# A fused vision block on one core: by-key scores in four PSUM banks, by-query scores in three, and a new order of the attention slots

## What is computed

```python
h = tok(x)                      # gray, two 3x3 Scharr convolutions, sum of absolutes / 2
n = layernorm(h)
q, k, v = n @ Wq + bq, n @ Wk + bk, n @ Wv + bv      # each in heads (b, n, 16, 16)
q, k = einsum("bnhe,ei->bnhi", q, Wp), einsum("bnhe,ei->bnhi", k, Wp)
scores = einsum("bnhi,bmhi->bnhm", q, k) / 4
h = h + einsum("bnhm,bmhe->bnhe", softmax(scores), v)
m = layernorm(h)
r = m + 0.5 * (silu(layernorm2(m) @ W1 + b1) @ W2 + b2)   # W1: 256x1024, W2: 1024x256, dequantised
out = h + r
```

## Time and profile before

| | us |
|---|---|
| median of 3 runs | 332.61 (329.96 to 335.14) |
| the profiled execution, its own time | 327.95 |
| its span in the trace | 326.2 |
| PE / PEld / DVE / ACT / POOL busy | 294.4 / 228.7 / 212.6 / 165.2 / 131.6 |

### The profile page before, as it was taken

How to read it: one execution, slowest core, us unless ns; L and a number is a source line. 1 busy time by engine, 2 the same in 40 slices (tenths; PEclk the granted TensorE clock), 3 DMA queues, 4 the chain that set the end, 5 groups by cost and what they waited for, 6 DMA issues and landing times.

```text
span 326.2 us, 6219 instructions
## 1 busy us (share of the span) xinstructions
PE 294.4 (90%) x2280; PEld 228.7 (70%) x2280; DVE 212.6 (65%) x423; ACT 165.2 (51%) x304; POOL 131.6 (40%) x250
## 2 busy tenths in 40 slices
PE   0599999999999997999999999788899999999996
PEld 0478888787767655565666656455699889999985
DVE  8979794846999676786777987431682563552422
ACT  1581534533323774767677766647434434444450
POOL 7423241502000108655747454326548769800000
PEclk9999999999999999999999999889999999999999
DMA  6985059999999676948990000000000100100201
GB/s 218 303 243 176 0 197 281 166 212 356 216 375 285 241 255 136 171 84 269 181 186 14 3 0 3 2 0 1 2 0 2 64 3 0 64 2 0 66 0 64
DMA packets 27911, 39.49 MB, mean 121 GB/s; under 512 B 4314, under 2 KB 14826, under 8 KB 27882
## 3 DMA queue, kind: packets, MB, share of 16 engines
q1 hardware_dynamic: 27720, 38.96, 45.2%
q10 hardware_dynamic: 162, 0.15, 0.1%
HBM read 24.42 MB, written 14.68 MB: 120 GB/s over the span
## 4 chain that ended last, share of the span: by engine, by line
PE 74%; DVE 14%; issue 5%; ACT 4%; POOL 1%; ACTq 0%; DVEq 0%; POOLq 0%
PE bank L1130 41%; PE bank L1244 9%; PE bank L1222 8%; PE bank L1227 4%; ACT probs L1037 3%; DVE negmax L841 3%; PE bank L1201 3%; PE bank L1262 3%; DVE qk_l L831 2%; PE bank L1254 2%; PE bank L1270 1%; DVE gray L718 1%; PE bank L1152 1%; DVE xn L806 1%; PE bank L1167 1%
## 5 line engine op out<-in xcount | busy, mean ns | idle before, releaser
L841 DVE TENSOR_REDUCE negmax<-bank 128x2 f32<-128x512 f32 x128 | 79.8, 682 | 15.7 <-PE bank L1201 15.7
L1037 ACT ACTIVATE probs<-bank 128x512 f32<-128x512 f32 x128 | 69.5, 595 | 35.5 <-PE bank L1227 33.6
L896 DVE TENSOR_TENSOR y_l<-yf,y_h 128x512 fp32r<-128x512 f32 x32 | 23.7, 742 | 39.1 <-ACT yf L1065 39.0
L1062 ACT ACTIVATE y_h<-bank,b1col 128x512 fp32r<-128x512 f32 x32 | 22.1, 689 | 48.5 <-PE bank L1130 48.4
L1130 PE MATMUL bank<-w_h,y_h 128*128 128x256 f32 x128 | 36.9, 288 | 2.5 <-DVE y_l L896 2.1
L1244 PE MATMUL bank<-probs,vals 128*32 128x256 f32 x512 | 35.1, 391 | 3.7
L1222 PE MATMUL bank<-negrow,pick 48*128 48x512 f32 x128 | 31.9, 495 | 7.0 <-ACT probs L1037 7.0
L1130 PE MATMUL bank<-w_l,y_h 128*128 128x256 f32 x128 | 36.2, 282 | 0.0
L1130 PE MATMUL bank<-w_h,y_l 128*128 128x256 f32 x128 | 36.2, 282 | 0.0
L1130 PEld LDWEIGHTS bank<-w_h,y_h 128*128 128x128 f32 x128 | 24.4, 190 | 4.6 <-DVE y_l L896 3.6
L1222 PEld LDWEIGHTS bank<-negrow,pick 48*128 48x128 f32 x128 | 12.0, 184 | 20.7 <-ACT probs L1037 15.4
(11 more groups left out here) (147 smaller groups left out, 627.6 us busy)
## 6 DMA issues: line engine op xcount, KB each, us to landing
qk_parts<-qk_h SPq DMA_DIRECT2D x32, 256.0 KB, 9.9
xr<-in_x SPq DMA_DIRECT2D x8, 768.0 KB, 8.4
qs<-qk_parts SPq DMA_DIRECT2D x16, 384.0 KB, 6.2
ks<-qk_parts SPq DMA_DIRECT2D x16, 384.0 KB, 7.8
qk_parts<-qk_l SPq DMA_DIRECT2D x16, 256.0 KB, 10.1
wraw<-in_L_ffn_fc_q SPq DMA_DIRECT2D x4, 512.0 KB, 3.9
wscale<-in_L_ffn_fc_scales SPq DMA_DIRECT2D x4, 512.0 KB, 7.3
out<-osb SPq DMA_DIRECT2D x16, 128.0 KB, 1.8
```

The source lines that it names most:

```text
L841: eng.tensor_reduce(negmax[:, b % 2, u, v], entry_bank(key)[:, :].rearrange("p (t k) -> p t k", t=NT), AX.X, ALU.max, negate=True).then_in ...
L896: eng.tensor_tensor(y_l[:, p % 2, f], yf[:, n % 2], y_h[:, p % 2, f].bitcast(fp32), ALU.subtract).then_inc(s_y, 1)
L1037: eng.activation(probs[:, n % PBUF], p2[n % 3][:, :], ACT.Exp).then_inc(s_exp, 1)
L1062: eng.activation(y_h[:, p % 2, f], src, ACT.Silu, bias=b1col[:, f:f + 1])
```

## The change

1. `p2` gets four banks (3 to 6), the ring three (0 to 2, n % 3). By-key scores of slot s now wait for the exponentials of slot s - 2, both heads, no longer for the first head of slot s - 1. All ring entries, those in the front too, wait for entry n - 3.
2. One by-query group (and its two reductions) a slot, not two groups in the even one. In the even slot it stands ahead of the by-key scores, in the odd one behind them: PE's row of a round is by-query, by-key, by-key, by-query, value products.
3. `copy_av` of a group stands on ACT behind the exponentials of the odd slot in which PE makes the group, no longer one slot later.
4. DRAM holds each high part once: two stores a tile, not three, and twelve loads of 16 partitions per half pair, not four of 48. Bytes loaded are the same.
5. The four loads of `fc1` weights are issued behind the last stores, before slot 0 of SP's loop, and wait only for the two stores under `wscale`; POOL's first step waits for all four. Before, they were issued from slot 2 on.
6. `fc1` product 1 goes to bank 1 and product 2 to bank 3, the other way round; product 2 waits for the last exponential.

```diff
-        p2 = bank[4:7]
+        p2 = bank[3:7]
...
         for s in range(END):
-            if s % 2 == 0:
-                for k in (s + AHEAD, s + AHEAD + 1):
-                    if k < SLOTS:
-                        head_entries(k)
+            if s + AHEAD < SLOTS:
+                head_entries(s + AHEAD)
...
-                r = n % 4
+                r = n % 3
...
-                for part, src in enumerate(((qk_h, qk_l, qk_h), (qk_h, qk_h, qk_l))[op]):
-                    eng.dma_start(qk_dram[p, op, m * P:(m + 1) * P, part, :], src[:, i, :].bitcast(fp32)).then_inc(s_store[i], 16)
+                for part, src in enumerate((qk_h, qk_l)):
+                    eng.dma_start(qk_dram[p, op, part, m * P:(m + 1) * P, :], src[:, i, :].bitcast(fp32)).then_inc(s_store[i], 16)
...
-                r, op, v = p % 2, k // 2, k % 2
-                src = qk_dram[p, op, m * P:(m + 1) * P].rearrange("(u v d) s t -> v (d s) u t", v=2, d=D)[v]
-                eng.dma_start((qs, ks)[op][HALF * v:HALF * v + SPLIT, r, m * 4:(m + 1) * 4, :].bitcast(fp32), src).then_inc(s_load[r][m], 16)
+                r = p % 2
+                op, slot, v = k // 6, k // 2 % 3, k % 2
+                part = ((0, 1, 0), (0, 0, 1))[op][slot]
+                dst = (qs, ks)[op]
+                first = HALF * v + slot
+                src = qk_dram[p, op, part, m * P:(m + 1) * P, :].rearrange("(u v d) t -> v d u t", v=2, d=D)[v]
+                eng.dma_start(dst[first:first + SPLIT - 2:3, r, m * 4:(m + 1) * 4, :].bitcast(fp32), src).then_inc(s_load[r][m], 16)
...
+            wait_filled(eng, ("qkv", PAIRS - 1, 0))
+            for i in range(2):
+                eng.wait_ge(s_store[i], 32 * PAIRS)
+            for part in range(4):
+                load_ffn(0, part)
...
-                if s >= 4 and s % 2 == 0:
-                    copy_av((s - 4) // 2)
+                if s % 2 == 1 and 3 <= s < SLOTS - 1:
+                    copy_av((s - 3) // 2)
...
-                if n >= 2:
-                    eng.wait_ge(s_exp, n - 1)
+                if n >= 4:
+                    eng.wait_ge(s_exp, n - 2)
...
             for s in range(END):
+                if s % 2 == 0 and s + AHEAD < SLOTS:
+                    scores_by_query(s + AHEAD)
                 if s < SLOTS:
                     scores_by_key(s)
-                if s % 2 == 0:
-                    for k in (s + AHEAD, s + AHEAD + 1):
-                        if k < SLOTS:
-                            scores_by_query(k)
+                if s % 2 == 1 and s + AHEAD < SLOTS:
+                    scores_by_query(s + AHEAD)
```

More of the change, by code:

```diff
@@ L298, in vit_tower_kernel @@
         N3_AT = {SLOTS - 9: (0, 0), SLOTS - 7: (0, 1)}
-        F1_AT = {SLOTS + (-5, -3, -1, 0)[i]: (i // KE, i % KE) for i in range(4)}
-        F1_AT.update({SLOTS + 2 + i: (2, i) for i in range(KE)})
+        F1_AT = {SLOTS + (-5, -3, -1, 0, 2, 3)[i]: (i // KE, i % KE) for i in range(6)}
         entries = []
@@ L337, in vit_tower_kernel @@
             held[r] = key
-        in_b = [[key for key in entries if ebank[key] == r and not (key[0] == "n3" and key[1] >= 1)][-1] for r in range(4)]
+        in_b = [[key for key in entries if ebank[key] == r and not (key[0] == "n3" and key[1] >= 1)][-1] for r in range(3)]
         def entry_bank(key):
@@ L357, in vit_tower_kernel @@
         LN_AT = (SLOTS - 24, SLOTS - 10)
[L360 removed]
+        F1_BANKS = (2, 1, 3)
         N3_MADE = {FT * (p - 1) + kf: (p, kf) for p in range(1, PAIRS) for kf in range(KE)}
@@ L425, in _ @@
                 stored(0, m)
-                for k in range(4):
+                for k in range(12):
                     load_qk(0, m, k)
@@ L453, in _ @@
                             eng.wait_ge(s_p2, max(s, UNITS * (2 * p - 3) + 4 * (m + 1)))
-                            load_qk(p, m, k)
-                if s in (2, 3, 5, 6):
-                    if s == 2:
-                        wait_read(eng, ("qkv", PAIRS - 1, 5))
-                        for i in range(4):
-                            eng.wait_ge(s_store[i], 48 * PAIRS)
-                    eng.wait_ge(s_p2, s)
-                    load_ffn(0, (2, 3, 5, 6).index(s))
+                            for i in range(3 * k, 3 * k + 3):
+                                load_qk(p, m, i)
                 if s in (23, 24):
@@ L600, in w1_step @@
                     eng.wait_ge(s_wraw, 16 * 4)
+                    if k == 0:
+                        for j in range(4):
+                            eng.wait_ge(s_store[j], 32 * PAIRS)
                     link(eng.tensor_scalar(full, wraw[:, cols], -128.0, 1.0, ALU.add, ALU.mult))
@@ L1036, in exp_head @@
                     eng.wait_ge(s_av, (n - PBUF) // 4 + 1)
-                eng.activation(probs[:, n % PBUF], p2[n % 3][:, :], ACT.Exp).then_inc(s_exp, 1)
+                eng.activation(probs[:, n % PBUF], p2[n % 4][:, :], ACT.Exp).then_inc(s_exp, 1)
             def neg_rows(b, half):
@@ L1214, in scores_by_key @@
                 if s < 2:
-                    for q in ((0, 1), (2,))[s]:
+                    for q in ((0,), (1, 2))[s]:
                         wait_read(eng, last_turns[q])
-                if n >= 2:
-                    eng.wait_ge(s_exp, n - 1)
+                if n >= 4:
+                    eng.wait_ge(s_exp, n - 2)
                 for v in range(2):
                     rows = slice(HALF * v, HALF * v + SPLIT)
-                    eng.matmul(p2[(n + v) % 3][:, :].rearrange("p (t n) -> p t n", t=NT), pick[rows, u % 4:u % 4 + 1].broadcast_to([SPLIT, P]),
+                    eng.matmul(p2[(n + v) % 4][:, :].rearrange("p (t n) -> p t n", t=NT), pick[rows, u % 4:u % 4 + 1].broadcast_to([SPLIT, P]),
                                negrow[rows, u // 4].unsqueeze(1).broadcast_to([SPLIT, NT, N]), start=True, stop=False)
```

25 lines of the change are left out of this document (12 added, 13 removed).

## The result

| | us |
|---|---|
| kernel before, median of 4 runs on the same chip | 331.28 (327.10 to 335.14) |
| changed kernel, median of 4 runs | 316.68 (315.09 to 317.30) |
| ratio, 95% interval | 0.9632 (0.9538 to 0.9725) |
| profiled execution of before / after, its own time | 327.95 / 317.30 |
| its span of before / after | 326.2 / 315.5 |

The change makes the kernel 3.7% faster; 317.1 was predicted, with 311 to 326 as the range. The ratio leaves out slow executions, those more than 1.5% above the fastest of their kernel: of the kernel before 332.61 and 335.14 here, of the changed one none, so that by it the change is worth 12.1 us (328.53, the mean of 329.96 and 327.10, times 0.0368), where the medians of all lie 14.6 us apart. The two profiled executions lie 10.65 us apart, and that is the number that the sum of the prediction, -15.3, was made against.

The account below looks back on a forecast made before the run. No engine was full; PE lost 0.38 and 0.20 us to two waits in each 3.27 us round. +1.4 - 10.1 - 1.6 - 5.0 = -15.3 us on 327.95 gives 312.65; factor 0.953 on 332.61 gives 317.1 us, range 311 to 326.

Parts of the forecast that it names:

- That is 13.3 us, or 1.57 less than 14.87: Slots 0 to 53: eight slots with `neg` and `out` take 13.3 us instead of 14.87; 1.5 was taken.
- There are 54 / 8 = 6.75 such spans: Slots 0 to 53: the eight-slot saving counted 6.75 times, -10.1 us (-6.1 to -15.5).
- Slot 0 begins +1.4 later: Front: by-query groups wait for DVE with three banks, so slot 0 starts 1.4 us later (0.4 to 3.1).
- rival C: Front's new waits or slot 55: PE's clock falls, 1.3 us each; five falls give 324 us; 7 in 100.
- Slots 54 to 63, -5.0: Slots without by-query scores: 2.3 us saved in slots 56 and 57, 3.15 in 58 to 63; 5.0 taken.
- The weight loads, -1.6: Slot 11: loads issued some 8 us earlier end PE's 1.58 us wait for POOL, -1.6 us (0 to -1.6).
- The profiled execution lies below the median of 332.61, so I apply the factor: Whole kernel: the profiled execution's factor of 0.953 applied to the median of 332.61, giving 317.1 us.
- Rival A: SP's loads in the front: the twelve do not overlap, slot 0 is delayed, 351 us; 5 in 100.
- The sign that I had set for A: Front: ACT's `qk_high` of pair 3 starting after 95 us would show that the twelve loads do not overlap.
- Rival B: Slots 0 to 53: ring of three holds PE in step with DVE, 10.8 us lost, 328 us; 13 in 100.
- Edits at nothing: Fewer store bytes, twelve loads for four and the swapped `fc1` banks: no change in time.
- 8 x 0.33 = 2.6 us later for the stores behind them: SP in the front: eight more load issues at 0.33 us each delay the following stores by 2.6 us.

Follow-up runs that it names:

- run 4: Changed kernel with row maxima taken over half of each row, the other half of every reduction left out: 305.10 us, ratio 0.9189.
- run 6: Changed kernel, new order and ring of three kept, but by-key scores rotate through three banks, bank 3 idle: 337.52 us, ratio 1.0270.
- run 5: Changed kernel with the front's ring entries in four banks, bank 3 going over to by-key scores in slot 0: 313.27 us, ratio 0.9527.
- run 1: Changed kernel with the DRAM layout of before, three stores a tile and four loads of 48 partitions: 314.94 us, ratio 0.9488.
- run 7: Kernel before with only the copies of the value products moved behind the odd slot's exponentials: 326.94 us, ratio 0.9905.
- Run 8: Kernel before with only the fc1 weight loads issued early, behind the last stores: 324.84 us, ratio 0.9898.
- run 9: Kernel before with both early fc1 weight loads and the value products' copy in the odd slot: 318.63 us, ratio 0.9687.

## Why the prediction held, and where its steps did not

The mechanism held, and the time by luck, since two errors cancelled. The gain was too large: 15.3 us against the profiled execution, where it was 10.7. And the base was too high: 332.61 was the median of three executions of which the ratio leaves out two. On the 328.53 of the other two the forecast factor would have given 313.2 us, 3.5 below what was measured. The factor itself, 0.953, lies just outside the measured 0.9538 to 0.9725. The 4.6 us between -15.3 and -10.7 are 2.5 in slots 0 to 53, 1.75 in the front and 0.36 in the last slots.

- **Rounds, "That is 13.3 us, or 1.57 less than 14.87": the mechanism right, the size a little off.** It is 13.55. Of my 13.3, PE's work and the wait for the copy of `neg` were 12.55 + 0.3; with halved reductions they come to 12.67 (run 4). DVE's part, two times 0.2, was too small: 13.55 - 12.67 = 0.88. A by-query group does not take "0.25 to 0.33" but 0.34, and 0.44 when it had to wait; by-key scores behind other 48-row products take 0.46, not 0.56.
- **"There are 54 / 8 = 6.75 such spans": not all are alike.** Slots 0 to 7 took 13.57 (102.65 to 116.22), without `out` entries and partly without a copy to await, and now take 12.81; they gave 0.76. Slots 40 to 47 now take 14.05, not 13.55, and gave 0.82. All rounds gave 7.9 us beside the 1.6 of slot 11 (9.54 between the by-key starts of slots 0 and 54, less 1.6), where I had 10.1. Of the 2.2 missing, 1.2 are the size (1.5 forecast for a span, 1.32 measured, 6.75 times) and 1.0 is the count. (The by-query group ahead of slot 0's by-key scores takes 0.34 of the 9.54, hence 9.20 in the stretches.)
- **The front, "Slot 0 begins +1.4 later": too small, by 1.75.** The 3.15 measured lies just above my bounds (0.4 to 3.1). The first wait was foretold to 0.1 us (82.15 forecast, 82.07 measured). That the clock would fall behind it I had only as a rival (C), at 1.3 us a fall, and not in this term: run 6, with the same wait and no fall, puts it at 1.5. Run 5 takes both away at once.
- **Slots 54 to 63, -5.0: measured -4.64.** Slots 58 to 63 came to 9.25, forecast 9.39. Slots 56 and 57 took 3.99, forecast 2.9; runs without the clock's fall show 2.71, and with what spills into slot 58 the fall costs 1.5 to 1.6 us (13.24 from slot 56 to `fc1`, 11.66 in run 1); rival C had 1.3 for one. In the traced execution it fell in two places, not in C's five. The Trainium skill (TensorE: Matmul & The Clock Gate, HAM oscillation) has the clock fall where waits leave gaps in PE's work. The front here, slot 11 in run 7 (0.66 behind a wait of 4.76 us) and slot 56 agree; run 1 at slot 56 and run 6 in the front, with the same waits of 1.51 and 1.71 us and no fall, show that a wait of that length need not bring it.
- **The weight loads, -1.6: right for the traced execution, too small for the others.** It was read from one execution, where the wait was 1.58 us. Run 8 alone gained 3.4 us by its ratio, run 7's trace shows the same wait at 4.76 with the clock's fall behind it, and both the spread and the wait go with the early loads. That this wait sets the spread of the kernel before is what runs 7, 8 and 9 point to; the longer executions of the kernel before itself were not traced, and which of their waits the clock fell behind is not shown. "The profiled execution lies below the median of 332.61, so I apply the factor" was the wrong way to carry the sum over: beside runs 8 and 9 the longer executions go with a lower granted clock, which is time lost in a few places and not a share of everything.
- **Rival A, twelve loads that do not overlap: did not come.** Loads of 128 KB land in 2.7 to 4.4 us, and nobody waits for them. By the Trainium skill (DMA: Bandwidth & Descriptors, Anatomy of one DMA) each would take about 2.3 us, an estimate from a fit that the page gives for transfers issued by GpSimd, while these are issued by SyncE. The trace's least is 2.7, and they overlap (an issue begins every 0.66 us on average in the front), so the fixed share of each costs no time here. Run 1 has four loads again and does not differ at an equal clock. The sign that I had set for A, ACT's `qk_high` of pair 3 after 95 us, did come up (95.22), but for another reason: ACT waited for PE there, whose front was late.
- **Rival B, PE in step with DVE: it came in part.** 0.88 us in eight slots, 6.75 times, are 5.9 us, of which 2.7 stood in the forecast (0.4 x 6.75); B wanted 10.8 more. Run 4 shows that this is what slots 0 to 53 now lose above PE's own work.
- **Edits at nothing** held in the time: layout (run 1), banks of `fc1` (`fc1` to `fc2` 6.87 in both). But "8 x 0.33 = 2.6 us later for the stores behind them" did not: they are 5.6 us later (80.89 to 86.44), since an issue now takes 0.60 us. That the long issues go by bytes no run shows, and these go against it: 0.60 us for 128 KB where it was 0.33 for 384. It cost nothing, as no engine waits for these stores now.

## What to carry to other kernels

Before a wait is priced from one trace, look at the spread of the runs and at the granted clock of each: here the kernel before gained 3.4 us from the end of a wait that the trace had at 1.58. Before a large change is built, try its small parts alone: moving the weight loads and the copy (run 9) came to 318.63 us beside the 317.19 of the whole. A bank moved from one ring to another is paid for in every place that the ring serves: the fourth by-key bank won in the slots and lost in the front, and giving the front its own division (run 5) kept the one and spared the other. Multiply a saving only by the spans that look like the one measured; the first and the last of a loop have other waits.
